# Score matmuls as three f32r passes, and q's bias ahead of its transposes

## The reference

```python
q = (query @ Wq.T + bq).reshape(B, T, H, D).transpose(0, 2, 1, 3)
k = (key @ Wk.T + bk).reshape(B, S, H, D).transpose(0, 2, 1, 3)
v = (value @ Wv.T + bv).reshape(B, S, H, D).transpose(0, 2, 1, 3)
scores = jnp.einsum('bhtd,bhsd->bhts', q, k) / np.sqrt(D)
scores = scores + causal[None, None]
attn = jax.nn.softmax(scores, axis=-1)
out = jnp.einsum('bhts,bhsd->bhtd', attn, v)
...
x = x + attention(layernorm(x), ctx, ctx)
gate, y = fp4_linear(h, w_gate), fp4_linear(h, w_up)      # h = layernorm(x)
x = x + fp4_linear(silu(gate) * y, w_down)
```

## Time and profile before

| | us |
|---|---|
| median of 3 runs | 1224.19 (1222.99 to 1224.69) |
| profiled execution | 1223.61 |
| its span (first to last instruction) | 1221.8 |
| PE / DVE / ACT / POOL busy | 1190.6 / 970.4 / 468.0 / 176.0 |
| attention block, about | 0 to 455 |
| iteration in the attention loop, about | 12.65 |
| mean granted TensorE clock | 0.993 |

### The profile page before, as it was taken

The page is one execution under the profiler, slowest core; times in us unless marked ns, Lnnn a source line. Parts: engine busy times, 40 slices in busy tenths (PEclk is TensorE's granted clock), DMA queues, the critical chain, the costliest instruction groups (busy, mean ns, idle before and its releaser), DMA issues.

```text
span 1221.8 us, 21262 instructions
## 1 busy us (share of the span) xinstructions
PE 1190.6 (97%) x6994; PEld 1085.7 (89%) x6994; DVE 970.4 (79%) x1705; ACT 468.0 (38%) x1141; POOL 176.0 (14%) x305
## 2 busy tenths in 40 slices
PE   7899999999999978899999999999999999999998
PEld 6688888888888868799999999999999999999997
DVE  6878888888888855788788788878878878877875
ACT  3556656565565632223223223223322322322321
POOL 3333333333333300000000000000000000000000
PEclk9999999999999999999999999999999999999999
DMA  6112121121332324323423522432342352253250
GB/s 231 29 53 78 52 75 54 57 73 52 115 100 88 119 93 178 63 55 78 84 54 63 100 54 54 99 63 54 91 72 54 74 89 54 56 101 60 54 90 28
DMA packets 91943, 94.33 MB, mean 77 GB/s; under 512 B 54513, under 2 KB 63905, under 8 KB 91784
## 3 DMA queue, kind: packets, MB, share of 16 engines
q1 hardware_dynamic: 91912, 93.95, 32.3%
HBM read 58.48 MB, written 23.94 MB: 67 GB/s over the span
## 4 chain that ended last, share of the span: by engine, by line
PE 59%; DVE 2%; issue 0%; ACT 0%; DVEq 0%; ACTq 0%
PE u_ps L173 7%; PE u_ps L174 6%; PE u_ps L175 6%; PE g_ps L173 6%; PE g_ps L174 6%; PE g_ps L175 6%; PE d_ps L1263 6%; PE d_ps L1264 6%; PE d_ps L1265 6%; PE xn_ps L311 1%; PE u_ps L1263 0%; PE u_ps L1265 0%; PE u_ps L1264 0%; DVE hquant_amax L118 0%; DVE hqf L1382 0%
## 5 line engine op out<-in xcount | busy, mean ns | idle before, releaser
L173 PE MATMUL g_ps<-wguh,xnh 128*128 128x352 f32 x512 | 168.5, 329 | 8.8 <-ACT silu L1302 3.7
L1368 DVE TENSOR_TENSOR hid<-u_ps,silu 128x352 f32<-128x352 f32 x128 | 66.6, 521 | 135.8 <-PE u_ps L175 135.8
L173 PE MATMUL u_ps<-wguh,xnh 128*128 128x352 f32 x512 | 168.5, 329 | 1.7 <-DVE hid L1368 1.7
L174 PE MATMUL u_ps<-wgul,xnh 128*128 128x352 f32 x512 | 165.8, 324 | 0.0
L174 PE MATMUL g_ps<-wgul,xnh 128*128 128x352 f32 x512 | 165.7, 324 | 0.0
L175 PE MATMUL g_ps<-wguh,xnl 128*128 128x352 f32 x512 | 165.6, 323 | 0.0
L175 PE MATMUL u_ps<-wguh,xnl 128*128 128x352 f32 x512 | 165.2, 323 | 0.0
L823 ACT ACTIVATE probs<-s_ps,nsmax 128x77 f32<-128x77 f32 x512 | 113.7, 374 | 99.1 <-DVE nsmax L912 99.1
L1302 ACT ACTIVATE silu<-g_ps 128x352 f32<-128x352 f32 x128 | 58.8, 459 | 220.5 <-PE g_ps L175 217.0
L1263 PE MATMUL d_ps<-wd,hqh 128*128 128x512 f32 x330 | 129.0, 391 | 0.0
L1264 PE MATMUL d_ps<-wd,hqh 128*128 128x512 f32 x330 | 128.9, 391 | 0.0
(11 more groups left out here) (146 smaller groups left out, 2544.2 us busy)
## 6 DMA issues: line engine op xcount, KB each, us to landing
scale_wide<-st_dram SPq DMA_DIRECT2D x248, 88.0 KB, 4.0
xin<-in_x_dram SPq DMA_DIRECT2D x32, 256.0 KB, 2.8
x_dram<-x SPq DMA_DIRECT2D x32, 256.0 KB, 2.0
xin<-x_dram SPq DMA_DIRECT2D x32, 256.0 KB, 2.9
out_dram<-y SPq DMA_DIRECT2D x32, 256.0 KB, 2.1
wd_dram<-wd_out SPq DMA_DIRECT2D x11, 512.0 KB, 3.9
wd<-wd_dram SPq DMA_DIRECT2D x1, 5632.0 KB, 17.1
w_in<-in_L_ffn_w_gate_dram SPq DMA_DIRECT2D x11, 256.0 KB, 2.9
```

The lines of the kernel that those rows point to most:

```text
L173: pe.matmul(out, lh, rh, start=(i == 0), stop=False)
L174: pe.matmul(out, lh, rl, start=False, stop=False)
L1368: dve.tensor_tensor(hid[:, c * GU_N:(c + 1) * GU_N], u_ps[:, c % 2, 0:GU_N], silu[:, c % 2, :], ALU.mult).then_inc(hid_ready, 1)
```

## The change

- The scores become three f32r passes per part: qh x kbh, qh x kbl, ql x kbh. qt and kbd are replaced by halves (qh, ql, kbh, kbl).
- q's bias: DVE adds it to q in its natural layout (a row broadcast, bq_all), before the transposes, in place of ACT's copy. In its order the addition moves from behind the piece's negated inverse to right behind the piece's block maximum. After the transposes ACT takes q's high half, as last before the piece's shift, and DVE the low half, where the bias addition stood. scores and project_q wait for both.
- The keys: one addition of DVE (kf), eight copies by ACT (kbh), eight subtractions by DVE (kbl); q's low half of tile 0 follows them. POOL clears two key tiles.
- wd_out has one buffer instead of two. The high half of a down piece waits until the piece before is stored.
- On SP, store_piece(t+3) moves from the end of loop body t to its start, ahead of load_piece(t+4).
- vext and some small tiles move into memory that the setup shares with the FFN's weights.

```diff
@@ SP, attention
-                sp.dma_start(wd_dram[:, :, c, :], wd_out[:, c % 2].bitcast(F32)).then_inc(wd_stored, 16)
+                sp.dma_start(wd_dram[:, :, c, :], wd_out[:].bitcast(F32)).then_inc(wd_stored, 16)
...
             for t in range(T):
 
+                if GU_PIECES <= t + 3 < PIECES:
+                    store_piece(t + 3)
                 if t + 4 < PIECES:
                     load_piece(t + 4)
                 store(t)
...
-                if GU_PIECES <= t + 3 < PIECES:
-                    store_piece(t + 3)
@@ TensorE, scores
-                    last = pe.matmul(out, qt[:, c, :], kbd[:, b, c, (h0 % 4) * CTX:(h0 % 4 + h1 - h0) * CTX],
-                                     start=not causal, stop=True)
+                    cols = slice((h0 % 4) * CTX, (h0 % 4 + h1 - h0) * CTX)
+                    pe.matmul(out, qh[:, c, :], kbh[:, b, c, cols], start=not causal, stop=False)
+                    pe.matmul(out, qh[:, c, :], kbl[:, b, c, cols], start=False, stop=False)
+                    last = pe.matmul(out, ql[:, c, :], kbh[:, b, c, cols], start=False, stop=True)
@@ ACT
-            def q_copy(t):
-                act.wait_ge(q_done, t + 1)
-                if reached(t):
-                    act.wait_ge(qT_done, t)
-                act.activation(q[:], q_ps[:], ACT.Copy).then_inc(q_copied, 1)
+            def q_high(t):
+                act.wait_ge(qT_done, t + 1)
+                if reached(t):
+                    act.wait_ge(s_done, S_BANKS * t)
+                act.activation(qh[:].rearrange("p c k -> p (c k)"), q_ps[:], ACT.Copy).then_inc(qh_ready, 1)
...
-                if valid(a):
-                    q_copy(a)
                 if valid(a - 2):
                     att_high(a - 2)
                 if valid(a - 1):
                     probs_copy(a - 1)
+                if valid(a):
+                    q_high(a)
                 if piece(n):
                     wquant.shift(act, n + 1)
...
+            def keys():
+
+                act.wait_ge(kf_ready, 1)
+                act.wait_ge(zeroed, 2)
+                for b in range(B):
+                    for i in range(4):
+                        r = slice(i * HD, (i + 1) * HD)
+                        last = act.activation(kbh[r, b, :, i * CTX:(i + 1) * CTX], kf[r, :, b * CTX:(b + 1) * CTX], ACT.Copy)
+                last.then_inc(kbh_ready, 1)
@@ DVE
             def q_bias(t):
-                dve.wait_ge(qT_done, t + 1)
+                if reached(t):
+                    dve.wait_ge(qT_done, t)
+                else:
+                    dve.wait_ge(bq_loaded, 16)
+                dve.wait_ge(q_done, t + 1)
+                dve.tensor_tensor(q[:], q_ps[:], bq_all[:], ALU.add).then_inc(q_biased, 1)
+
+            def q_low(t):
+                dve.wait_ge(qh_ready, t + 1)
                 if reached(t):
                     dve.wait_ge(s_done, S_BANKS * t)
-                dve.tensor_tensor(qt[:], q_ps[:].rearrange("p (c k) -> p c k", k=P), bcast(bqc[:], P), ALU.add).then_inc(q_ready, 1)
+                dve.tensor_tensor(ql[:].rearrange("p c k -> p (c k)"), q_ps[:],
+                                  qh[:].rearrange("p c k -> p (c k)").bitcast(F32), ALU.subtract).then_inc(ql_ready, 1)
...
+                if valid(a):
+                    q_bias(a)
                 if valid(a - 2):
                     att_low(a - 2)
...
                 if valid(a):
-                    q_bias(a)
+                    q_low(a)
                 if piece(n):
                     wquant.make_magic(dve, n + 1)
```

More of the change, by code:

```diff
@@ L199, in __init__ @@
             self.cin, self.ctxT = row(("cin", [CTX, B, E]), ("ctxT", [P, EC, B, CTX]))
-            self.bv_all, self.bias_nat = row(("bv_all", [CTX, E]), ("bias_nat", [EC, 2, P]))
+            self.bv_all, self.bias_nat, self.vext, self.kf, self.bkc = row(
+                ("bv_all", [CTX, E]), ("bias_nat", [EC, P]), ("vext", [CTX, B, 2, HALF_HEADS, VW]),
+                ("kf", [P, EC, B * CTX]), ("bkc", [P, EC]))
 class Shared:
@@ L354, in attention @@
         w_nat, wkt, wvt, cin, ctxT = k.setup.w_nat, k.setup.wkt, k.setup.wvt, k.setup.cin, k.setup.ctxT
-        bv_all, bias_nat = k.setup.bv_all, k.setup.bias_nat
+        bv_all, bias_nat, vext, kf, bkc = (k.setup.bv_all, k.setup.bias_nat, k.setup.vext, k.setup.kf, k.setup.bkc)
         with ExitStack() as sctx:
@@ L372, in attention @@
         ath, atl = sb("ath", [P, EC, P], F32R), sb("atl", [P, EC, P], F32R)
-        wd_out = sb("wd_out", [P, 2, 2, E], F32R)
+        wd_out = sb("wd_out", [P, 2, E], F32R)
         q_ps = ps("q_ps", [P, 512])
@@ L471, in _ @@
             sp.dma_start(cin[:], ctx_in.rearrange("b s d -> s b d")).then_inc(in_loaded, 16)
-            for i, row in enumerate((bq, bk)):
-                sp.dma_start(bias_nat[:, i, :], row.rearrange("(c p) -> c p", p=P)).then_inc(in_loaded, 16)
+            sp.dma_start(bias_nat[:], bk.rearrange("(c p) -> c p", p=P)).then_inc(in_loaded, 16)
             load(0)
             load_weight(1, Wq)
+            sp.dma_start(bq_all[:], bq.rearrange("(a n) -> a n", a=1).to_broadcast(bq_all.shape)).then_inc(bq_loaded, 16)
             load_piece(0)
@@ L601, in biases @@
                         pe.transpose(kp[:, b, c * P:c * P + CTX], cin[:, b, c * P:(c + 1) * P], ident[0:CTX, 0:CTX])
-                for i in range(2):
-                    last = pe.transpose(s_ps[:, 2, 8 * i:8 * i + EC], bias_nat[:, i, :], ident[0:EC, 0:EC])
-                last.then_inc(small_done, 1)
+                pe.transpose(s_ps[:, 2, 0:EC], bias_nat[:], ident[0:EC, 0:EC]).then_inc(small_done, 1)
             def keys():
-                pe.wait_ge(small_ready, 3)
+                pe.wait_ge(small_ready, 2)
                 pe.wait_ge(wth_ready, EC)
@@ L790, in piece_high @@
                     c = n - GU_PIECES
[L791 to L795, removed]
+                    if reached(c):
+                        act.wait_ge(wd_stored, 16 * c)
+                    dst = wd_out[:, 0, :].rearrange("p (c k) -> p c k", k=P)
                 else:
@@ L862, in _ @@
             wquant.shift(act, 1)
-            q_copy(0)
+            keys()
             weight_high(2)
+            q_high(0)
             piece_high(0, False)
@@ L943, in piece_low @@
                     c = n - GU_PIECES
-                    high, low = (wd_out[:, c % 2, i, :].rearrange("p (c k) -> p c k", k=P) for i in range(2))
+                    high, low = (wd_out[:, i, :].rearrange("p (c k) -> p c k", k=P) for i in range(2))
                 else:
@@ L1007, in biases, with keys_low @@
                                 kp[:].rearrange("p b (c s) -> p b c s", s=P)[:, :, :, 0:CTX]).then_inc(small_ready, 1)
-                dve.tensor_copy(bqc[:], s_ps[:, 2, 0:EC]).then_inc(small_ready, 1)
-                dve.tensor_copy(bkc[:], s_ps[:, 2, 8:8 + EC]).then_inc(small_ready, 1)
+                dve.tensor_copy(bkc[:], s_ps[:, 2, 0:EC]).then_inc(small_ready, 1)
             def keys():
                 dve.wait_ge(k_done, 1)
-                dve.wait_ge(zeroed, 1)
-                dve.wait_ge(small_ready, 3)
+                dve.wait_ge(small_ready, 2)
+                dve.tensor_tensor(kf[:], kp[:].rearrange("p a (c s) -> p (a c) s", c=2)[:, :, 0:B * CTX],
+                                  bcast(bkc[:], B * CTX), ALU.add).then_inc(kf_ready, 1)
+            def keys_low():
+                dve.wait_ge(kbh_ready, 1)
                 for b in range(B):
@@ L1018, in keys @@
                         r = slice(i * HD, (i + 1) * HD)
[L1019 to L1023, removed]
+                        cols = slice(i * CTX, (i + 1) * CTX)
+                        last = dve.tensor_tensor(kbl[r, b, :, cols], kf[r, :, b * CTX:(b + 1) * CTX],
+                                                 kbh[r, b, :, cols].bitcast(F32), ALU.subtract)
+                last.then_inc(kbl_ready, 1)
             def values(b):
```

33 lines of the change are left out of this document (19 added, 14 removed).

## The result

The changed kernel takes 1293.11 us (median of 4, 1291.79 to 1293.39), the kernel before 1223.83: 1.056 times as long, 95% interval 1.0546 to 1.0582. The forecast was 1291. Two of its terms were off by more than 5 us each and made up for one another, so the stages are what has to be compared.

The account below looks back on a forecast made before the run. TensorE was taken to pace the attention loop at 12.65 us, DVE's own loop close behind at 12.4 to 12.5. Setup 3, DVE cycle 7, bubble 54, clock 3, iteration 31 0.5: 1223.6 + 67.5 = 1291 us, range 1270 to 1313.

Parts of the forecast that it names:

- What bounds the kernel: Attention loop: TensorE sets the pace at 12.65 us; DVE's loop through POOL and ACT needs 12.4 to 12.5 by itself.
- part 2: DVE's order in the attention loop: bias addition ahead of the chain makes the cycle 13.03 us, +0.39, 18 times, +7.0 us.
- Rival (b): Attention loop: bubble hidden, DVE's wait of 1.30 us absorbs the new operation, TensorE sets 12.48; 1220 us, chance 0.04.
- Part 1: Scores on TensorE: three f32r passes take 1.91 us against 2.08, saving 0.17 an iteration.
- The upper bound: Scores: a narrow f32r pass costs as much as the fp32 product of its width, 0.26 us; scores 2.81 us.
- rival (c): Scores: each narrow f32r pass costs its upper bound, TensorE's cycle is 13.38 us; 1297 us in all, chance 0.08.
- Part 3: SP's queue, down pieces: load behind the store leaves DVE a 5.05 us bubble per piece; +5.44, ten times, +54 us.
- Rival (a): Down pieces: the bubble is hidden because the load is early enough, DVE's cycle alone counts; 1238 us, chance 0.07.
- Part 4: TensorE's clock: half clock after many bubbles, mostly hidden by 1.3 us of slack; +3 us in all (0 to 24).
- three us at half speed: TensorE after a bubble: three us at half clock add about 1.5, a cost of 0.2 to 0.3 an iteration.
- Rival (d): TensorE's clock: half speed for all its work on DVE's path, up to 2.4 us an iteration; 1312 us, chance 0.1.
- Part 5: Setup and ends: key halves and q(0)'s low half cost +3 us with iterations 1 and 2 (0 to 6); iteration 31 +0.5.

Follow-up runs that it names:

- the kernel with the load first: The changed kernel with load_piece(t+4) issued first on SP and store_piece(t+3) right behind it: 1235.19 us, 1.0096 times the kernel before.
- the last version: The kernel with the load first, q's bias added after its transposes, batch 1's keys split at setup's end, q(0) copied after batch 0's keys: 1225.21 us.

## Why the prediction was right

**What bounds the kernel, part 2.** Right, and now shown by intervention. DVE's loop through POOL and ACT was only just under TensorE's time; 0.61 us ahead of it lengthened the cycle to 13.11 (forecast 13.03) from 12.65. The two places of an extra operation of the same length, 12.64 against 13.17, show the rule by itself, and 13.17 less 0.6 puts the loop's own length at 12.6, 0.1 under TensorE and above the 12.4 to 12.5 of the prediction. Rival (b), that the wait absorbs the new work, falls for the order of this change. In the order in which both operations stand in the wait it is nearly true: the cycle is 12.59, where (b) had 12.48.

**Part 1.** 1.94 us for the scores, forecast 1.91. The narrow passes take 0.113 us, near the 0.109 of the row chosen for them. The upper bound, and with it rival (c), falls. The gap of the Trainium skill, "TensorE: Matmul & The Clock Gate", section Back-to-back issue gap, would give 1.58; the rows show 0.14 for 308 columns, not far from its 0.131, and 0.113 for 154, where it gives 0.067. The Trainium skill itself calls this the isolated gap, and says that for small N it counts too little in a stream in which every matmul loads weights. The trace agrees: 0.113 against 0.067. For large N the Trainium skill says that the formula counts too much, and gives about 0.131 us for 512 columns in such a stream; there the trace does not agree, for the f32r matmuls of 512 columns in the projections start every 0.23 us.

**Part 3.** The mechanism was right and its size too large. The wait was 4.57 us (41.1 over 9), forecast 4.97 (5.05 less the overlap). That forecast has a slip: from 312.56 to 312.87 is 0.31, and it entered 0.2. The load landed in 3.7 us by the median, not 4.0, and SP's step from store to load took 0.62 in 348.63 to 349.25, not 0.73. Besides, the down stage's cycle without a bubble is 12.88, not 13.03. So with the clock held up the ten iterations took 48.7 us more than before (175.4 against 126.8), where 54 were forecast. Rival (a) falls: without the bubble the kernel takes 1235, which is what (a) said within 3 us, but the bubble was not hidden.

**Part 4.** The term that was mis-sized. Forecast +3, measured 8.7 in the loop. The step that failed is "three us at half speed", taken for every iteration. Six of the ten half-clock stretches were 3.4 us long and four were 6.8. Against the 17.54 us of an iteration with the bubble filled, the six cost 0.36 each, not far from the forecast's 0.2 to 0.3, and the four 1.64 each: 2.2 + 6.5 = 8.7. In the iteration with the stretch from 334.30 to 341.10, TensorE takes 6.48 us from the transposes of q to the first scores (335.25 to 341.73) and 3.63 at full clock (260.78 to 264.41), 2.85 more. A second, smaller fault is the place. The prediction let the delay meet DVE at the maxima of the scores, with 1.3 us of slack. The residual stands before them in DVE's queue and needs the output projection. There the trace shows the waits, 1.64 us in the long case, and there the slack is about 1.1: in the kernel with the load first the projection ends at 210.77 and the residual starts at 212.29, and where DVE waits, it starts 0.44 after the projection's end. Rival (d) had the path wholly at half clock in all ten iterations, at 2.4 each; that came near the truth in four of them. The Trainium skill, same page, section Why this matters for your kernels, warns of idle gaps for this reason, and the trace agrees: 0.51 behind the bubbles, 1.00 where they were filled.

**Part 5.** +4.5 against +3. Kernels with the same setup code reach the first x1 store between 69.03 and 72.70 us, and the more half clock TensorE had up to it, the later it is: 0.95 on average at 69.03 and 69.20, 0.93 at 69.38 and 70.59 (the changed kernel), 0.88 at 72.70. The kernel before had 0.95 and 66.06. So at the same clock the new setup costs 3.0, the forecast, and the other 1.5 goes with the clock, which the prediction had not counted in the setup. How the 3.0 divides between the key copies, the subtractions and q's low half is not shown.

The errors, forecast less measured: -1.5 in the setup, +5.3 in the bubble and the cycle under it, -5.7 in the clock, -0.7 in iteration 31, where filling the bubble gave 1.0 back. In iterations 3 to 20 the sum was right, but spread otherwise: nothing in the first two, 0.44 in each of the others. That the total was 2 us off is luck in part: 5.3 too much stood against 5.7 too little. The signs that the prediction named were there: waits for w_in of 4.5 us, x1 stores 18.4 us apart, TensorE waiting 0.3 for the bias addition (forecast 0.5), the fall of the clock.

What stays open: why the half clock lasted 6.8 us behind some bubbles and 3.4 behind others, and 3.4 us of the last version's setup, beyond what its clock explains.

## What to carry to other kernels

Read an engine's own loop from one of its instructions to the same one in the next iteration, and subtract only the waits that another engine's pace makes: an engine idle a fifth of the time was 0.1 us from setting the pace here. An operation in a wait that the engine's own chain makes left the cycle as it was; ahead of that chain one of the same length added 0.5 of its 0.6 us. And on a DMA queue, ask of every wait what stands behind it: a store that waits for the last result of an iteration must not stand in front of the load that the next one begins with.

## What the runs showed of the hardware

A bubble on TensorE costs more than its length here: 3.7 to 4.6 us of standing still brought 3.4 or 6.8 us at 1.2 GHz behind it, 0.4 or 1.6 us of an iteration; 180 matmuls without any use made the kernel 11 us faster. The load behind a 512 KB store landed in 3.7 us, 0.3 less than in the kernel before, where transfers of x were issued just ahead of the two. And two kernels that differ only in later code reached their first x1 store 3.7 us apart (69.03 and 72.70), because TensorE ran 9.8 us of the setup at half clock in the one and at full clock in the other.
